# State-space rows of a macaron block: products for B, C and delta one step earlier, a norm in another place of ScalarE's order, two more inputs on GpSimd

## The reference, cut to what matters

```
x = x + 0.5 * ffn(norm(x));  x = x + ssm(norm(x));  x = x + 0.5 * ffn(norm(x))
```

```
x, z  = gelu(conv4(h @ W_in))            # two halves of 128 channels
dt, B, C = split(x @ W_xproj)            # 8, 16, 16
delta = softplus(dt @ W_dt + b_dt)
dA[l] = exp(delta[l] * A);  dBu[l] = delta[l] * B[l] * x[l]
h[l]  = dA[l] * h[l-1] + dBu[l];  y[l] = sum_n h[l, n] * C[l, n] + x[l] * D
out   = concat(y, z) @ W_out
```

## Time and profile before

| what | value |
|---|---|
| median of three runs | 863.77 us |
| profiled execution | 864.46 us, span 862.7 us |
| busy share of the span | PE 97%, DVE 79%, POOL 75%, ACT 65% |
| granted TensorE clock, mean | 0.995 |
| state-space stage | 335 to 550 us |
| scans in it | 64 of 2.25 to 2.29 us |
| inputs on VectorE | 50 of 1.21 us |
| inputs on GpSimd | 14 of 2.37 us |

### The profile page before, as it was taken

One profiled execution on the slowest core, in us unless ns is written; L12 is line 12 of the kernel. 1 busy time (PEld: TensorE's weight loads), 2 busy tenths in 40 slices (PEclk: granted clock), 3 DMA queues, 4 the chain that ended last, 5 costly groups with the idle time before them and its releaser, 6 DMA issues. The chain is left out here.

```text
span 862.7 us, 12807 instructions
## 1 busy us (share of the span) xinstructions
PE 833.8 (97%) x3906; PEld 639.7 (74%) x3906; DVE 682.4 (79%) x1264; ACT 562.0 (65%) x1057; POOL 648.5 (75%) x476
## 2 busy tenths in 40 slices
PE   8999999999999999999999998999999999999997
PEld 7678777887877786667666665787887888788885
DVE  6969767776976578999999999787876977776664
ACT  6575565565566657899999894365565556555553
POOL 6958675776685757999999999766776677676765
PEclk9999999999999999999999998999999999999999
DMA  8644474445434242566456554436366436535440
GB/s 216 213 128 115 137 197 109 139 124 157 122 102 129 94 147 98 221 226 216 164 198 226 178 202 148 161 85 180 106 181 175 122 126 159 156 112 174 136 122 25
DMA packets 127286, 130.03 MB, mean 151 GB/s; under 512 B 59497, under 2 KB 83185, under 8 KB 127217
## 3 DMA queue, kind: packets, MB, share of 16 engines
q1 hardware_dynamic: 104512, 123.96, 46.6%
q10 hardware_dynamic: 22704, 5.25, 2.8%
HBM read 119.74 MB, written 9.44 MB: 150 GB/s over the span
## 5 line engine op out<-in xcount | busy, mean ns | idle before, releaser
L817 POOL TENSOR_TENSOR act_lo<-act,act_hi 128x512 fp32r<-128x512 f32 x288 | 372.3, 1298 | 188.7 <-ACT act_hi L928 186.6
L921 ACT ACTIVATE bank<-bank 128x512 f32<-128x512 f32 x252 | 146.8, 582 | 234.0 <-PE bank L1255 224.4
L1151 DVE TENSOR_TENSOR sg<-bank,c_ring 128x512 f32<-128x512 f32 x252 | 172.6, 685 | 97.1 <-ACT bank L921 94.7
L1251 PE MATMUL bank<-x_parts,w_hi 128*128 128x512 f32 x572 | 231.5, 405 | 3.1 <-DVE sg L1151 1.9
L1129 DVE SCALAR_TENSOR_TENSOR act<-sg,bank 128x512 f32<-128x512 f32 x288 | 197.8, 687 | 41.9 <-PE bank L1255 21.1
L1255 PE MATMUL bank<-x_parts,w_hi 128*128 128x512 f32 x572 | 226.0, 395 | 0.0
L1252 PE MATMUL bank<-x_parts,w_lo 128*128 128x512 f32 x572 | 226.0, 395 | 0.0
L928 ACT ACTIVATE act_hi<-act 128x512 fp32r<-128x512 f32 x286 | 178.3, 624 | 0.4 <-PE bank L1227 0.4
L1251 PEld LDWEIGHTS bank<-x_parts,w_hi 128*128 128x128 f32 x572 | 107.4, 188 | 35.9 <-issue 4.8
L1255 PEld LDWEIGHTS bank<-x_parts,w_hi 128*128 128x128 f32 x572 | 107.4, 188 | 26.2
L1252 PEld LDWEIGHTS bank<-x_parts,w_lo 128*128 128x128 f32 x572 | 107.5, 188 | 25.6 <-issue 1.6
(11 more groups left out here) (190 smaller groups left out, 1023.7 us busy)
## 6 DMA issues: line engine op xcount, KB each, us to landing
c_ring<-c_dram SPq DMA_DIRECT2D x252, 256.0 KB, 3.6
c_ring<-c_dram SPq DMA_DIRECT2D x64, 512.0 KB, 4.3
b_slots<-c_dram SPq DMA_DIRECT2D x14, 512.0 KB, 4.9
y_dram<-out_t SPq DMA_DIRECT2D x56, 64.0 KB, 2.8
y_tok<-y_dram SPq DMA_DIRECT2D x14, 256.0 KB, 3.7
xt_dram<-xn ACTq DMA_DIRECT2D x40, 64.0 KB, 3.4
xt<-xt_dram ACTq DMA_DIRECT2D x10, 256.0 KB, 3.3
out<-x_sb SPq DMA_DIRECT2D x7, 256.0 KB, 2.3
```

The costliest lines, as they stand in the source:

```text
L817: self.nc.gpsimd.tensor_tensor(m["act_lo"][:, g % LAG], m["act"][:, g % ACTS], m["act_hi"][:, g % LAG].bitcast(FP32), ALU.subtract).then_i ...
L921: nc.scalar.activation(self.h_bank[:, g % 2], self.h_bank[:, g % 2], ACT.Silu).then_inc(self.sg_ready, 1)
L1151: nc.vector.tensor_tensor(m["sg"][:, g % 2], silu, weight, ALU.mult).then_inc(self.w_done, 1)
L1251: nc.tensor.matmul(dst, m["w_hi"][:, k, n, :], x_hi, start=True, stop=False)
```

## The change

Four things change place or number; the arithmetic is the same.

- `MOVED`: row 0 has pairs 5 and 6 (slots 0 and 1) as moved pairs, and row 6 has pairs 2 and 4, so 16 in all. In row 0 SyncE issues slot 0 behind the C of pair 1 and slot 1 behind the C of pair 3, and GpSimd multiplies them before products 2 and 4.
- The products for B and C and for delta of row i+2 now stand at step 7 of row i, behind the sum of states, and wait there for u and z; the low half's product stays at step 0 but ahead of the sum of states. For row 1 they stay.
- The norm is applied at step 3, between the copy of y and the decays of pair 4, and not at step 4. The first norm of the second expert stage takes that place in row 5, which needs GpSimd's norm block behind pair 38 and not pair 44.
- In row 6 the place is taken by the next piece of that stage (a copy).

```diff
--- before.py
+++ after.py
@@ -40,7 +40,7 @@
 
 TURNED = 0, 1, 2, 3, 4, 5, 6
 ADDED = ((),) * 7 + ((PAIRS - 2, PAIRS - 1),)
-MOVED = ((None, 6),) + ((2, 4),) * 5 + ((4,), (2, 4))
+MOVED = ((5,6),)+((2,4),)*7
 SLOTS = 2
 MULT_STEP = 1
 LOW_STEP = 0
@@ -222,7 +222,7 @@
                     if g in HEAD_ACT:
                         next(head)
                 front = f2.act_front_pieces(ae)
-                for g, _ in enumerate(mamba.act_pairs(ae)):
+                for g, _ in enumerate(mamba.act_pairs(ae, front)):
                     if g in FRONT_ACT:
                         next(front)
                 for _ in front:
@@ -281,8 +281,8 @@
 HEAD_ACT = (106, 107, 109, 113, 116, 117, 122, 125, 137)
 HEAD_PE = (108, 111, 112, 115, 121, 124, 130)
 FRONT_DVE = {54: 2, 56: 1, 57: 1, 58: 1, 59: 1, 60: 1, 61: 1}
-FRONT_POOL = (44, 50, 55, 58)
-FRONT_ACT = (46, 48, 50, 52, 54, 56, 61, 62)
+FRONT_POOL = (38, 50, 55, 58)
+FRONT_ACT = (50, 52, 54, 56, 61, 62)
 FRONT_PE = (49, 51, 52, 60, 61, 63)
 
 
@@ -1460,9 +1460,9 @@
                              self.c_dram[i, NS + 2 * n:NS + 2 * n + 2].rearrange("s l -> (s l)").partition_broadcast(P)
                              ).then_inc(self.c_loaded[n % RING], 16)
                 if i + 1 < BATCH:
+                    if i == 0 and n in (1, 3):
+                        self.load_slot(sp, 0, n // 2)
                     if n == 3:
-                        if i == 0:
-                            self.load_slot(sp, 0, 1)
                         self.store_rows(sp, i + 1)
                     if n == 5:
                         sp.wait_ge(self.c_stored, 16 * (i + 2))
@@ -1514,8 +1514,8 @@
                     if n == 7:
                         pool.wait_ge(self.du_ready, i + 2)
                         self.pool_input(pool, i + 1, 0)
-                if i == 0 and n == 4:
-                    self.pool_input(pool, 0, 1)
+                if i == 0 and n in (2, 4):
+                    self.pool_input(pool, 0, n // 2 - 1)
                 if i and n == MULT_STEP:
                     self.pool_input(pool, i, 1)
                 if n == 6 and i == 2:
@@ -1666,7 +1666,7 @@
         self.norm.act_apply(ae, BATCH + 2)
         yield
 
-    def act_pairs(self, ae):
+    def act_pairs(self, ae, front):
         self.nc.scalar.preload_act_table_set("exp_and_others")
         ae.wait_ge(self.setup.a_step, 2)
         self.act_decays(ae, 0)
@@ -1685,14 +1685,18 @@
                     self.act_delta(ae, i + 1)
                 if n == 3 and i:
                     (self.act_turned_y if i - 1 in TURNED else self.act_y)(ae, i - 1)
+                if n == 3 and i and i + 3 < BATCH:
+                    self.norm.act_apply(ae, BATCH + i + 3)
+                if n == 3 and BATCH - 3 <= i < BATCH - 1:
+                    next(front)
                 if RING <= g + 1 < ALL_PAIRS and self.moved(g + 1):
                     self.act_decays(ae, g + 1)
                 if RING <= g + 2 < ALL_PAIRS and not self.moved(g + 2):
                     self.act_decays(ae, g + 2)
                 if n == 3 and i - 1 in TURNED:
                     self.act_back_y(ae, i - 1)
-                if n == 4 and i + 3 < BATCH:
-                    self.norm.act_apply(ae, BATCH + i + 3)
+                if n == 4 and i == 0:
+                    self.norm.act_apply(ae, BATCH + 3)
                 if 1 <= i <= 5 and n == 4:
                     if i == 1:
                         ae.wait_ge(self.f1.x_added, BATCH)
@@ -1967,20 +1971,24 @@
                 g = i * PAIRS + n
                 if 1 < g < ALL_PAIRS - 1:
                     self.pe_spread(pe, g + 1)
+                if n == LOW_STEP and 0 < i < BATCH - 1:
+                    self.pe_low(pe, i + 1, front[:, 0, :])
                 if SUM_LAG <= g <= ALL_PAIRS - PAIRS + 1:
                     self.pe_add_states(pe, g - SUM_LAG)
                 if g > ALL_PAIRS - PAIRS:
                     self.pe_add_states(pe, g - LAST_LAG)
 
                 step = n if i else n - 2
-                if step == 0 and i + 1 < BATCH:
-                    if i == 0:
-                        pe.wait_ge(self.f1.acc_read, BATCH)
-                    self.pe_bc(pe, i + 1, front[:, 0, :])
-                    need(pe, self.z_gated, i)
-                    self.pe_delta(pe, i + 1, front[:, 1, :])
-                if step == LOW_STEP and i + 1 < BATCH:
-                    self.pe_low(pe, i + 1, front[:, 0, :])
+                if i == 0 and step == 0:
+                    pe.wait_ge(self.f1.acc_read, BATCH)
+                    self.pe_bc(pe, 1, front[:, 0, :])
+                    self.pe_delta(pe, 1, front[:, 1, :])
+                if i == 0 and step == LOW_STEP:
+                    self.pe_low(pe, 1, front[:, 0, :])
+                if n == 7 and i + 2 < BATCH:
+                    self.pe_bc(pe, i + 2, front[:, 0, :])
+                    pe.wait_ge(self.z_gated, i + 1)
+                    self.pe_delta(pe, i + 2, front[:, 1, :])
                 if i + 2 < BATCH:
                     if step == 1:
                         pe.wait_ge(self.low_done, i + 1)
```

## The result

The changed kernel takes 865.44 us (median of 20 runs) against 864.07 us for the kernel before (20 runs): ratio 1.0016, 95% interval 1.0009 to 1.0022. By that ratio it is 1.4 us slower, where the forecast was 1.8 us faster and the range ended at 864.9. Two of the 20 executions of the changed kernel stand apart (916.0 us at a mean granted clock of 0.86, and 2024.4 us); the ratio leaves them out, and the median of the other 18 is 865.25 us. The profiled execution took 866.17 us, its span is 864.4 us.

The account below looks back on a forecast made before the run. GpSimd's queue was taken as the bound from 344 us to the routing step, 1.8 us earlier: 864.46 less 1.8 is 862.7 profiled, less 0.69 for the median is 862.0 us. The range was 860.4 to 864.9.

Parts of the forecast that it names:

- Waits for ScalarE at pair 2: Rows 1 to 5: VectorE's waits for decays (0.59 us a row, 0.91 in row 1) go, 2.7 us by waits.
- TensorE's new stand: Row's end: TensorE stands until ScalarE has made u and z; 1.2 us of cover at pair 1's spread, priced at 0.
- GpSimd's queue as the bound: From 344.35 GpSimd runs without slack up to the routing step, which begins at 522.0, 1.8 us earlier than before.
- the second part: Products for B, C, delta one step earlier, norm in ScalarE's wait: must give at least 1.5 us for the sum to hold.
- the sign of being wrong: Waits of GpSimd for scans in rows 1 to 4 would show that VectorE is the bound.
- Slot 0 and C in row 0: Row 0: slot 0 lands in 3.6 us, C costs nothing, scan 6 waits 0.4 us, some 0.8 us of gain stay.
- The input of row 6: One of two inputs moved to GpSimd: each saves VectorE 1.29 us and costs GpSimd 2.323 us.
- L1037: Row 7: VectorE, about 4.8 us early, waits some 3 us for GpSimd's g_in; scan 57 comes 1.8 us early.
- After scan 57: Pair 59's spread moves from 528.66 to 526.9; the slow-clock loss of 2.2 us is taken again.
- rival 4: The slow stretch grows by 2.2 us, giving 864.2; chance 0.24 together with rival 3.
- Rival 2: TensorE's stand at the row's end costs 0.5 to 1.0 us in each of 6 rows, middle 865.7; chance 0.14.
- rival 3: No measurable change: GpSimd's chain starts later or waits for C in row 0, 863.3; chance 0.24 together with rival 4.

Follow-up runs that it names:

- e1: Changed kernel with the GpSimd inputs and slot loads of the kernel before, so only the new order of products and norm: 864.29 us, ratio 1.0004.
- e3: Changed kernel with one convolution tap matmul of TensorE moved behind the spread of pair 8i+6 (the later tap): 863.89 us, ratio 0.9995 to the kernel before.
- e6: Changed order of products and norm with the later convolution tap, but the 14 GpSimd inputs of the kernel before: 862.03 us, ratio 0.9971.
- e4: Changed kernel with row 0 as before (pair 6 alone moved), row 6 still with two inputs: 865.63 us, ratio 1.0020 to the kernel before.
- e10: Changed kernel with only pair 4 of row 6 moved, as before, so 15 inputs on GpSimd: 863.27 us, ratio 0.9998 to the kernel before.
- e14: Changed kernel in which GpSimd multiplies only 64 of 1024 columns of row 6's new input: 863.68 us, ratio 0.9999 to the kernel before.
- e2: Kernel before with all 16 inputs on GpSimd, its order of products and norm unchanged: 865.04 us, ratio 1.0012.
- e13: Kernel before with small zero-adding matmuls filling TensorE's waits between 519 and 526 us: 864.43 us, ratio 1.0008.
- e16: Kernel before with only row 0's second input moved to GpSimd (pairs 5 and 6), order unchanged: 863.59 us, ratio 1.0002.
- e5: Kernel before with the convolution tap of step 4 (rows 1 to 5) moved behind the spread of pair 8i+6: 863.36 us, ratio 0.9988.
- e11: Changed kernel with later tap, row 6's second input back on VectorE, and small zero-adding matmuls in TensorE's waits: 862.10 us, ratio 0.9985 to the kernel before.
- e12: Changed kernel with small zero-adding matmuls in TensorE's waits between 519 and 526 us: 865.39 us, ratio 1.0020 to the kernel before.

## Why the prediction was wrong, point by point

**Waits for ScalarE at pair 2.** They went, as forecast. The step that failed is "the waits ... go, if nothing else comes late", with TensorE's new stand priced at 0. What came late was not the stand (scan 25 had no wait) but the spread of pair 8i+6, at the end of 11.2 us of full TensorE. The forecast followed the chain that VectorE waited for and not the second one from the same scan. VectorE's gain of 2.7 us came out as a loss of 0.5 us up to scan 57 (e1), and returned, in part, only when a matmul left the stretch (e3; e6 has scan 57 at relative 189.44, 1.6 us earlier than in the kernel before). In row 1 TensorE's stand, priced at 0, did come late (scan 9).

**GpSimd's queue as the bound.** Right, and the largest term (69 operations of 2.323 us, three norms, seven du) was right to 0.1 us. It was wrong that nothing would stop it. The forecast itself said that the second part had to give 1.5 us for product 38 to be in time; it gave nothing, and product 38 waited 1.53 us. That is the sign of being wrong that the forecast itself had named: GpSimd waits for a scan in row 4, so VectorE is the bound up to there. The 3.15 us by which the ranking missed the forecast all come of this step, since GpSimd would have waited at product 38 all the longer without its delays in row 0.

**Slot 0 and C in row 0.** Slot 0 was priced at the shortest landing, 3.6 us; it took 4.3 us, and its input began 0.76 us later than forecast; C was priced at 0 and cost GpSimd 0.83 us (its range was 0 to 2.4). Scan 6 waited 1.23 us, not 0.4, and row 0 gained nothing, not 0.8 us. With row 0's input out, however, the kernel is not faster (1.0020 against 1.0016), so this term did not decide: product 38 waits either way (1.59 us in e4).

**The input of row 6.** The forecast booked both inputs with one sum. Row 6's is the one that costs: 1.0016 with it, 0.9998 without it (e10), 0.9999 with GpSimd's part of it cut (e14); with the later tap 0.9995 against 0.9968 and 0.9972. It puts 2.32 us on an engine that had 1.09 us of gap left there (e10), and the 1.29 us that it saves on VectorE go into a wait of 2.5 us.

**L1037.** The wait was forecast at 3 us and is 2.54 us, but that is luck. VectorE was to come 4.8 us early and g_in 1.8 us early; they came 1.2 us early and 1.4 us late. Both terms miss by over 3 us, and only their difference was nearly right.

**After scan 57.** "I take the same loss again" was short: the wait before it was 3.67 us, as forecast, the slow stretch longer (6.36 us for 5.48), and 0.75 us more was lost up to scan 63. That is rival 4, at a third of its size. The rule of the Trainium skill (TensorE: Matmul & The Clock Gate, section "HAM oscillation — how this bites in real kernels"), that a group of matmuls behind waits starts slow, agrees with the clock of 0.53 behind that wait. That the slow stretch was certain is not borne out: in e2 TensorE waited 1.06, 1.90 and 2.15 us at the same three places, and its clock stayed at 1.00. Closing earlier waits with small matmuls brought the clock to 1.00 here but no shorter time.

**The rivals.** Rival 2 named the right sign and engine, but its chain came late only at row 1 and not in each of six rows. Both delays of rival 3 came (0.76 and 0.83 us), but e4 shows that they are not what made the kernel slower. No rival had a second TensorE chain behind the first.

## What to carry to other kernels

Before a wait is priced as a gain, follow from the scan that frees a bank every engine that works without a gap until it next hands something over, not only the one waited for: here a second chain ended 0.1 us behind the first, and 0.6 us of wait only changed its name. An operation moved to another engine costs there what the gaps up to the next hand-over do not take up (here 2.32 less 1.09 us), so it can pay only where that engine waits for others, and not where others wait for it. A delay ahead of a wait of the same engine costs nothing up to that wait: look for the last wait ahead of the hand-over, and count from there. When a wait is moved ahead and the work of its engine stays the same, look for it further on.

## What the hardware showed that was not expected

TensorE's clock fell in different places of the same stage: around 530 us in most profiled executions, in row 6 in e13, in both places in e16, nowhere in e2, e5, e11 and e12. Each time it was the level of 1.2 GHz (0.50). The waits before it do not tell whether it falls: TensorE's last three waits before the spread of pair 59 were 1.07, 1.90 and 1.12 us in the kernel before, where it fell, and 1.06, 1.90 and 2.15 us in e2, where it did not. Small matmuls of K 64 (28 records, 3.39 us for 14) in the waits before held it at full clock in row 7 and made no median shorter.
